# A graph layer and an expert layer on one core: norm sums moved to VectorE, rank sums added in DRAM, five chunk buffers instead of six

## The chip, the cores and the metric

The kernel runs on one core of a Trainium2 chip. The metric is device time in microseconds of that core. A core has five engines with instruction queues of their own: PE (TensorE: matmuls), DVE (VectorE), ACT (ScalarE), POOL (GpSimd) and SP (SyncE, which issues transfers here and computes nothing). An engine runs its queue in order; engines wait for one another through semaphores. DMA engines, 16 of them, move data between DRAM and the on-chip buffer (SBUF).

## The reference

`x` is 10000 x 128, `adj` is 10000 x 10000, both float32, and two layers follow each other, each added to `x`:

```
h = item_feat @ W_item.T + b_item
x = x + relu(adj @ h + layernorm(x) @ W_user.T + b_user)
z = layernorm(x)
probs = softmax(z @ gate_w + gate_b)          # 8 experts, the best two of each row count
x = x + sum over the two: prob * (gelu(z @ W1[e] + b1[e]) @ W2[e] + b2[e])
```

`adj` alone is 400 MB, and it is read once. The hidden width of an expert is 256.

## The kernel before, in words

**Blocks and chunks.** The 10000 rows of the result are cut into 20 blocks (`BLOCKS`) of 500 rows, a block's 9984 columns of `adj` into 26 chunks (`CH`) of 3 x 128. The loop variable n runs over all 520 chunks (`NCH`), c = n % 26 is the chunk in its block, and every engine's program is this one loop with small work hung into it at fixed places. A chunk is 750 KB. SP loads it into one of six buffers (`raw`, `load_raw`), which is free again when VectorE has subtracted the chunk that was in it six chunks ago (`lo_made`). ScalarE rounds it to a short format (`a_hi`, L742, three buffers), VectorE makes the rest, `a_lo = raw - a_hi` (L952, two buffers), and TensorE adds nine matmuls of 500 columns into one bank: hi x h_hi, hi x h_lo, lo x h_hi (L496, L497, L501). A short matmul for the last columns (L510) and one for the user weights (L512) end a block.

**Small work behind a block.** While block b is summed, block b-1 is finished, at places named by constants (`X1_AT` = 1, `BN2_AT` = 4, `LG_AT` = 11, ...): relu and residual (L977), turning into token order, statistics (`stats1`, `stats2`, L971 and L987), the factors of both norms (`rs`, made on Pool by `rstd`, eleven small instructions L1304 to L1320, the last but two a power of -1/2), the norms on ScalarE (L758, L787), gate logits on VectorE (L998 to L1006), the power of the softmax on Pool (L1324), the two best experts (`top`), and a slot for each row and rank (`slots`). `bn` and `rs` have one buffer.

**Scatter, fill, tiles, send.** Blocks 0 to 16 go the sparse way. Pool scatters each block's rows to expert order in DRAM (`zs`), eight indirect DMAs of 125 rows (L1346). Blocks 0 to 11 are group 0, blocks 12 to 16 group 1. When a group is scattered, VectorE writes a table of tiles, SP fills the ends of the experts' regions (`fill_end`, L379, waits for all of the group's scatters), and then 31 and 17 tiles of 512 rows (`NTG`) go through the expert's two matmul layers between the chunks. A tile's load (`load_zt`, L352) waits for the fills; its weights come by `load_w`. At a tile's end Pool sends its rows, scaled by their probability, to DRAM (`rr`, four indirect DMAs, L1355); VectorE waits with the output of tile k until the sends of tile k-2 have landed. The tiles start at `W1_AT`: the first one of group 0 at chunk 352.

**Dense steps.** Blocks 17 to 19 are run through all eight experts after the last chunk, 24 steps d with no sorting: first layer, GELU on ScalarE (L857), a scaling by the gate on VectorE (L1172), rounding (L866), rest (L1176), second layer. The GELU's output has two buffers (`dg`).

**Combine.** `out_s` holds the sparse blocks' residual, `rr` each row's two ranks. For each of the 17 sparse blocks SP loads 512 rows of `out_s` into SBUF (`comb_load`), Pool adds both ranks by accumulating DMAs (`comb_add`, L1336), and SP stores it (`comb_store`, L367). All this stands after the last chunk, beside the dense steps, and SP's `out_store` of the dense blocks (L372) stands in the same queue.

Of the kernel before, what the change touches and what calls it, by code (L numbers as in the profile page):

```python
# [23 lines left out]
RAW, HIS, LOS = 6, 3, 2  # L24
# [51 lines left out]
W_LOAD = [0, 0] + [w + (6 if o + 2 < NTG[0] else 4) for o, w in enumerate(W1_AT[:NT - 2])] + [NCH - 3, NCH - 2]  # L76
ZT_LOAD = [0, 0] + [max(W1_AT[k - 2] + 3, FILL_AT[k >= NTG[0]] + E // 2) for k in range(2, NT)]
COMB_AT = [p if p < GROUPS[1][0] else p + 3 for p in range(S)]
COMB_OUT = [6 + p if p < GROUPS[1][0] else p + 10 for p in range(S)]
# [22 lines left out]
def build(nc, adj, adj_tail, x_tok, x_t, feat_t, feat_tail, wi_t, bb, bsel_d, wu_t, gate_w, gate_b,  # L102
          w12, b12, b2, ident_d, tri_d, w8_d, base_d, dest_d, sel_d, ints_d, out_s, out_d, zs, rr):
    ctx = ExitStack()
    with ctx:
# [27 lines left out]
        bias = sb("bias", [P, 4, 3])  # L133
# [35 lines left out]
        consts = sb("consts", [P, 4, 2 * SUBS])  # L169
# [5 lines left out]
        tsl = sb("tsl", [P, 2, SUBS, E])  # L175
        idx = sb("idx", [P, 2 * SUBS], I32)
# [36 lines left out]
        bn1_made, bn2_made, rs_step, rs_made = sem("bn1_made"), sem("bn2_made"), sem("rs_step"), sem("rs_made")  # L213
        ln1_normed, ln1_turned, ln1_copied, ln2_normed = (
# [31 lines left out]
        def dg(d):  # L246
            return g[:, 0:2 * UB] if d % 2 else flat[:, 0:2 * UB]
# [47 lines left out]
        def _(sp):  # L295
# [31 lines left out]
            def load_w(o):  # L327
# [27 lines left out]

            def comb_load(p):
                if p == 0:
                    sp.wait_ge(lo_made, NCH)
                    sp.wait_ge(x1_stored, 16 * S)
                if p >= CB:  # L360
                    sp.wait_ge(comb_stored[p % CB], 16 * (p // CB))
                sp.dma_start(comb(p), out_s[p * T:(p + 1) * T, :].rearrange("(p s) d -> p (s d)", s=SUBS))\
                    .then_inc(comb_loaded[p % CB], 16)

            def comb_store(p):
                sp.wait_ge(comb_added[p % CB], 32 * (p // CB + 1))
                sp.dma_start(out_s[p * T:(p + 1) * T, :].rearrange("(p s) d -> p (s d)", s=SUBS), comb(p))\  # L367
                    .then_inc(comb_stored[p % CB], 16)
# [19 lines left out]
            for n in range(NCH):  # L388
# [57 lines left out]
            for j in range(ND + 5):  # L446
                for p in range(S):
                    if COMB_OUT[p] == j:
                        comb_store(p)
                for p in range(S):  # L450
                    if COMB_AT[p] == j:
                        comb_load(p)
# [5 lines left out]
            for i in range(CB):  # L458
                sp.wait_ge(comb_stored[i], 16 * ((S - 1 - i) // CB + 1))
# [275 lines left out]
        def _(act):  # L735
# [84 lines left out]
            def gelu(k):  # L820
# [3 lines left out]
                for h in range(2):  # L824
                    fn(g[:, h * T:(h + 1) * T], hid[h][:, :], ACT.Gelu, bias=bias[:, k % 4, h:h + 1])\  # L825
# [8 lines left out]
            def y_evac(k):  # L834
# [3 lines left out]
                fn(yt[:, :], y[0][:, :], ACT.Identity, bias=bias[:, k % 4, 2:3]).then_inc(yt_made, 1)  # L838
# [9 lines left out]
            def dense_gelu(d):  # L848
# [5 lines left out]
                if d >= 2:  # L854
                    act.wait_ge(gl_made, o - 1)
# [89 lines left out]
        def _(dve):  # L945
# [34 lines left out]
            def stats2(p):  # L980
# [7 lines left out]
                last.then_inc(bn2_made, 1)  # L988

# [231 lines left out]
            for n in range(LAST):  # L1221
# [3 lines left out]
                if b == 0:  # L1225
# [6 lines left out]
                    if c == 8:  # L1232
# [4 lines left out]
                        nc.vector.tensor_copy(base[:, :], base0[:, 0:E]).then_inc(base_set, 1)  # L1237
                    if c == 16:
# [244 lines left out]
```

## Time and profile before

| | |
|---|---|
| median of 3 runs | 1539.0 us (1538.3 to 1539.04) |
| the profiled execution | 1538.6 us, span 1536.8 us |
| PE busy, DVE busy | 1469.6 us (96%), 1248.4 us (81%) |
| ACT busy, POOL busy | 1095.3 us (71%), 885.7 us (58%) |
| moved by DMA | 498.06 MB, mean 324 GB/s |

The span runs from the first to the last instruction; what lies around it is 1.8 us. Busy time of PE is modelled at the ends of matmuls, which overlap: a matmul's row says 0.39 us while the next one starts 0.23 us after it. So idle time of TensorE is read from the distance between the starts of rows, not from its busy share.

### The profile page before, as it was taken

Reading aid. Unit: us, or ns where it says so; the run is one execution under the profiler, and the core shown is the slowest. Engines: PE = TensorE matmul, PEld = TensorE weight load, DVE = VectorE, ACT = ScalarE, POOL = GpSimd, SP = SyncE. Lnnn points to the kernel's source line nnn. Section 1 sums busy time; section 2 is a strip of 40 time slices with the busy share of each in tenths; the row PEclk is TensorE's granted clock in tenths of the full one; section 3 lists DMA queues with packets and bytes.
Section 4 is the critical chain, followed back from the end, with each engine's and each line's share of the span. In section 5 each row is a group of like instructions: output and inputs, shape, how many; then the busy total and the mean of one; then the engine's idle time right before and its main releaser. Section 6 shows DMA issues by size and latency. Waiting matters only on the chain.

```text
span 1536.8 us, 20551 instructions
## 1 busy us (share of the span) xinstructions
PE 1469.6 (96%) x6682; PEld 1172.5 (76%) x6682; DVE 1248.4 (81%) x1627; ACT 1095.3 (71%) x1162; POOL 885.7 (58%) x630
## 2 busy tenths in 40 slices
PE   8999999999999999999998798999999999999997
PEld 6777787877877877778776587888888887877664
DVE  4778788888887887888888687889898988888775
ACT  4567677677677676776774677788887878788664
POOL 0105735637557457456364148777887887587662
PEclk9999999999999999999999899999999999999999
DMA  8879999999999999999997987889898899888399
GB/s 327 303 302 348 366 360 361 377 345 344 378 347 354 364 345 364 363 344 384 338 350 262 371 315 271 332 327 337 327 335 326 327 338 331 287 274 283 110 219 229
DMA packets 141720, 498.06 MB, mean 324 GB/s; under 512 B 33024, under 2 KB 39120, under 8 KB 141614
## 3 DMA queue, kind: packets, MB, share of 16 engines
q1 hardware_dynamic: 119694, 466.12, 82.3%
q0 software_dynamic: 21920, 30.64, 7.6%
q8 instruction: 53, 0.87, 0.2%
q14 instruction: 53, 0.43, 0.1%
HBM read 460.22 MB, written 36.31 MB: 323 GB/s over the span
## 4 chain that ended last, share of the span: by engine, by line
PE 49%; DVE 15%; POOL 14%; issue 8%; ACT 7%; DMA 5%; SPq 2%; POOLq 0%; ACTq 0%; DVEq 0%
PE p_agg L501 13%; PE p_agg L496 11%; PE p_agg L497 11%; DVE s_a_lo L952 9%; ACT s_a_hi L742 4%; POOL s_rs L1316 3%; DMA s_raw<-rr 3%; POOL s_rs L1304 2%; POOL zs L1346 2%; POOL s_rs L1312 1%; POOL s_rs L1305 1%; PE p_hid L478 1%; PE p_hid L589 1%; PE p_hid L591 1%; PE p_hid L590 1%
## 5 line engine op out<-in xcount | busy, mean ns | idle before, releaser
L952 DVE TENSOR_TENSOR s_a_lo<-s_raw,s_a_hi 128x1500 fp32r<-128x1500 f32 x520 | 885.8, 1718 | 139.4 <-PE p_agg L501 84.4
L742 ACT ACTIVATE s_a_hi<-s_raw 128x1500 fp32r<-128x1500 f32 x520 | 750.1, 1454 | 207.9 <-PE p_agg L501 184.9
L496 PE MATMUL p_agg<-s_a_hi,s_h_hi 128*128 128x500 f32 x1560 | 630.6, 404 | 10.2 <-ACT s_a_hi L742 10.1
L497 PE MATMUL p_agg<-s_a_hi,s_h_lo 128*128 128x500 f32 x1560 | 611.7, 392 | 0.0
L501 PE MATMUL p_agg<-s_a_lo,s_h_hi 128*128 128x500 f32 x1560 | 449.3, 396 | 33.9 <-DVE s_a_lo L952 31.0
L1346 POOL DMA_INDIRECT zs<-s_rows,s_idx x136 | 231.9, 1705 | 306.3 <-DVE s_idx L1080 211.8
L501 PEld LDWEIGHTS p_agg<-s_a_lo,s_h_hi 128*128 128x128 f32 x1560 | 290.2, 190 | 120.2 <-DVE s_a_lo L952 63.3
L496 PEld LDWEIGHTS p_agg<-s_a_hi,s_h_hi 128*128 128x128 f32 x1560 | 297.4, 191 | 75.3 <-ACT s_a_hi L742 17.9
L497 PEld LDWEIGHTS p_agg<-s_a_hi,s_h_lo 128*128 128x128 f32 x1560 | 297.3, 191 | 57.9 <-issue 3.2
L1355 POOL DMA_INDIRECT rr<-s_ysb,s_dests x192 | 277.4, 1445 | 102.7 <-issue 53.1
L1324 POOL TENSOR_TENSOR s_gt<-s_ebase,s_gt 125x32 f32<-125x32 f32 x20 | 130.8, 6538 | 37.2 <-DVE s_gt L1006 37.1
L1304 POOL TENSOR_TENSOR s_rs<-s_bn 125x8 f32<-125x8 f32 (+1 forms) x21 | 42.2, 2010 | 113.6 <-DVE s_bn L971 104.3
L1154 DVE TENSOR_TENSOR s_gl<-s_g,s_gh 128x1024 fp32r<-128x1024 f32 x48 | 58.8, 1226 | 51.3 <-ACT s_gh L832 51.3
L825 ACT ACTIVATE s_g<-p_hid,s_bias 128x512 f32<-128x512 f32 x96 | 60.6, 684 | 48.5 <-PE p_hid L591 48.5
L832 ACT ACTIVATE s_gh<-s_g 128x1024 fp32r<-128x1024 f32 x48 | 50.9, 1060 | 9.3 <-PE p_y L607 8.1
L1316 POOL TENSOR_TENSOR s_rs<-s_rs,s_consts 125x8 f32<-125x8 f32 (+1 forms) x21 | 55.7, 2655 | 1.6
L838 ACT ACTIVATE s_yt<-p_y,s_bias 128x512 f32<-128x512 f32 x48 | 32.6, 680 | 31.4 <-PE p_y L607 31.4
L787 ACT ACTIVATE s_rows<-p_agg,s_rs 125x128 f32<-125x128 f32 x80 | 30.0, 456 | 34.1 <-POOL s_rs L1320 34.1
L1336 POOL DMA_DIRECT2D s_raw<-rr x34 | 31.0, 1134 | 32.8 <-DMA s_raw<-out_s 16.7
L746 ACT ACTIVATE s_h_hi<-p_hid 128x384 fp32r<-128x384 f32 x26 | 12.8, 491 | 41.2 <-PE p_hid L478 41.2
L589 PE MATMUL p_hid<-s_zh,s_wt 128*128 128x512 f32 (+1 forms) x102 | 41.7, 409 | 0.4 <-ACT s_g L857 0.4
L818 ACT ACTIVATE s_zh<-p_tp 128x512 fp32r<-128x512 f32 x48 | 28.2, 587 | 19.0 <-PE p_hid L591 17.2
(214 smaller groups left out, 1478.6 us busy)
## 6 DMA issues: line engine op xcount, KB each, us to landing
s_raw<-adj SPq DMA_DIRECT2D x520, 750.0 KB, 6.6
s_wraw<-w SPq DMA_DIRECT2D x56, 256.0 KB
s_zt<-zs SPq DMA_DIRECT2D x48, 264.0 KB, 3.1
s_raw<-rr POOLq DMA_DIRECT2D x34, 256.0 KB, 6.7
s_xtok<-x_tok SPq DMA_DIRECT2D x20, 256.0 KB, 5.6
s_xt<-x_t SPq DMA_DIRECT2D x20, 250.0 KB, 6.7
zs<-s_early SPq DMA_DIRECT2D x18, 264.0 KB, 5.7
out_s<-s_x1s SPq DMA_DIRECT2D x17, 256.0 KB, 6.5
```

What stands on the lines that cost most here:

```text
L496: mm(o, h_hi[:, k * D:(k + 1) * D], hi, start=(k == 0), stop=False)
L497: mm(o, h_lo[:, k * D:(k + 1) * D], hi, start=False, stop=False)
L501: last = mm(o, h_hi[:, k * D:(k + 1) * D], a_lo[:, n % LOS, j * UB:(j + 1) * UB], start=False, stop=False)
L742: fn(a_hi[:, n % HIS, :], raw[:, n % RAW, :], ACT.Copy).then_inc(hi_made, 1)
L825: fn(g[:, h * T:(h + 1) * T], hid[h][:, :], ACT.Gelu, bias=bias[:, k % 4, h:h + 1])\
L952: tt(a_lo[:, n % LOS, :], raw[:, n % RAW, :], a_hi[:, n % HIS, :].bitcast(F32), ALU.subtract)\
L1154: tt(gl[:, :], g[:, :], gh[:, :].bitcast(F32), ALU.subtract).then_inc(gl_made, 1)
L1304: tt(row[0], even, odd, ALU.add)
L1316: tt(row[1], row[5], mhalf, ALU.pow).then_inc(rs_step, 1)
L1324: gp.tensor_tensor(gt[0:TS, 2, :], ebase[0:TS, :], gt[0:TS, 1, :], ALU.pow).then_inc(ez_made, 1)
L1346: gp.indirect_dma_start(out=zs[:, :], out_offset=bass.IndirectOffsetOnAxis(ap=idx[0:TS, j:j + 1].bitcast(U32), axis=0), in_=rows[k][0:TS, ...
L1355: gp.indirect_dma_start(out=rr[:, :], out_offset=bass.IndirectOffsetOnAxis(ap=dests[:, k % XR, s:s + 1].bitcast(U32), axis=0), in_=yrows(k ...
```

## The change

Seven things are changed at once.

1. `RAW` goes from 6 to 5, and the kernel is built with 8192 instead of 4096 bytes for the descriptors that Pool writes.
2. `rstd` is split. VectorE makes the variance in six instructions (`variances`, chunk 4) and the shift in one (`shifts`, chunk 7); Pool makes only the power (`power_of_rs`).
3. The small work stands three to four chunks earlier: logits at 8 instead of 11, softmax at 12 instead of 16, slots and scatter at 17 instead of 21.
4. Fills start two chunks earlier, the first tile of group 0 five chunks earlier (347 instead of 352); the steps between tiles of group 1 are 2.41 chunks instead of 2.12. The tiles' biases have six buffers instead of four, and the loads of weights and rows stand at other chunks.
5. Scatters take 128 rows instead of 125. The three more go to spare rows of `zs`, whose numbers a new input `idx` holds.
6. The combine doesn't go through SBUF. Pool adds `rr` onto `out_s` in DRAM, two blocks of group 0 to a DMA, six DMAs for each rank, issued behind the sends of twelve tiles of group 1; group 1 follows at the end in two DMAs of five blocks.
7. The GELU's output of the dense steps has three buffers.

```diff
-RAW, HIS, LOS = 6, 3, 2
+RAW, HIS, LOS = 5, 3, 2
-X1_AT, X1T_AT, BN2_AT, BN1_AT, X1S_AT, LG_AT, LN2_AT = 1, 1, 4, 5, 4, 11, 12
-TAILHI_AT, TAILLO_AT, SOFT_AT, TOP1_AT, TOP2_AT, LN1_AT = 9, 10, 16, 17, 18, 15
-PREFIX_AT, LN1T_AT, SLOT_AT, LN1C_AT = 19, 17, 21, 20
-TABLE_AT = (21, 22, 23)
+X1_AT, X1T_AT, X1S_AT, BN1_AT, BN2_AT, FIN_AT, LG_AT, LN2_AT = 1, 1, 4, 3, 4, 7, 8, 9
+TAILHI_AT, TAILLO_AT, SOFT_AT, TOP1_AT, TOP2_AT, LN1_AT = 6, 7, 12, 13, 14, 11
+PREFIX_AT, LN1T_AT, SLOT_AT, LN1C_AT = 15, 13, 17, 16
+TABLE_AT = (17, 18, 19)
-FILL_AT = [(hi + 1) * CH + 6 for lo, hi in GROUPS]
-FIRST_W1 = [at + E // 2 + 4 for at in FILL_AT]
+FILL_AT = [(hi + 1) * CH + 4 for lo, hi in GROUPS]
+FIRST_W1 = [at + E // 2 + 1 for at in FILL_AT]
...
+            def variances(j):
+                lo, hi = SUBS if j == 0 else 0, SUBS if j == BLOCKS else 2 * SUBS
+                if j < BLOCKS:
+                    dve.wait_ge(bn1_made, j + 1)
+                if j >= 1:
+                    dve.wait_ge(bn2_made, j)
+                row = [rs[0:TS, i, lo:hi] for i in range(RS)]
+                even, odd = bn[0:TS, lo:hi, 1], bn[0:TS, lo:hi, 4]
+                tt(row[3], even, odd, ALU.subtract)
+                tt(row[4], bn[0:TS, lo:hi, 2], bn[0:TS, lo:hi, 5], ALU.add)
+                tt(row[0], even, odd, ALU.add).then_inc(rs_step, 1)
+                dve.wait_ge(rs_step, 2 * j + 1)
+                nc.vector.tensor_scalar(row[4], row[4], 1.0 / D, EPS, ALU.mult, ALU.add)
+                nc.vector.scalar_tensor_tensor(out=row[3], in0=row[3], scalar=0.25, in1=row[3],
+                                               op0=ALU.mult, op1=ALU.mult).then_inc(rs_step, 1)
+                dve.wait_ge(rs_step, 2 * j + 2)
+                tt(row[5], row[3], row[4], ALU.add).then_inc(var_made, 1)
+            def shifts(j):
...
+                dve.wait_ge(pow_made, j + 1)
...
-            def rstd(j):
...
+            def power_of_rs(j):
...
+                gp.tensor_tensor(rs[0:TS, 1, lo:hi], rs[0:TS, 5, lo:hi], mhalf[0:TS, lo:hi], ALU.pow)\
+                    .then_inc(pow_made, 1)
...
+            def add_rank(i, k):
+                blocks = GROUPS[0][1] // PAIRS
+                first, last = (i * blocks, (i + 1) * blocks) if i < PAIRS else GROUPS[1]
+                if k == 0:
+                    pool.wait_ge(rr_zeroed, 16 * 3)
+                    pool.wait_ge(x1_stored, 16 * last)
+                    for j in range(2):
+                        pool.wait_ge(sent[j], 16 * SUBS * tiles_of(j, NTG[0] if i < PAIRS else NT))
+                else:
+                    pool.wait_ge(rank0_added, 16 * (PAIRS + (i == PAIRS)))
...
+                gp.dma_start(out, new, max_dma_last_dim=8192, accum_op=ALU.add).then_inc((rank0_added, rank1_added)[k], 16)
...
             def dg(d):
-                return g[:, 0:2 * UB] if d % 2 else flat[:, 0:2 * UB]
+                return (flat[:, 0:2 * UB], g[:, 0:2 * UB], flat[:, 2 * UB:4 * UB])[d % 3]
...
-                if d >= 2:
-                    act.wait_ge(gl_made, o - 1)
+                if d >= 3:
+                    act.wait_ge(gl_made, o - 2)
...
-                            in_=rows[k][0:TS, s, :], in_offset=None).then_inc(scattered, 16)
+                            in_=rows[k][:, s, :], in_offset=None).then_inc(scattered, 16)
...
                         send(k)
-                        if k == NT - 3:
-                            rstd(BLOCKS)
+                        i = k - NTG[0] - 1
+                        if 0 <= i < 2 * PAIRS:
+                            add_rank(i % PAIRS, i // PAIRS)
+            power_of_rs(BLOCKS)
+            power(BLOCKS - 1)
+            add_rank(PAIRS, 0)
+            add_rank(PAIRS, 1)
...
-    nc = bacc.Bacc("TRN2", target_bir_lowering=False, num_devices=1, dynamic_dma_scratch_size=4096)
+    nc = bacc.Bacc("TRN2", target_bir_lowering=False, num_devices=1, dynamic_dma_scratch_size=8192)
```

## Rows read from the trace of the kernel before

**Rows 1.** Windows: us, busy (x) PE PEld DVE ACT POOL, PEclk, DMA share, GB/s

```profile
402.00:461.70 59.70, 57.55 (x261) 46.48 (x260) 50.37 (x61) 42.21 (x38) 33.88 (x21) 1.00 0.96 358
406.00:426.00 20.00, 20.00 (x97) 16.82 (x96) 17.39 (x19) 14.38 (x12) 15.89 (x13) 1.00 0.99 377
...
1433.50:1536.80 103.30, 88.98 (x346) 58.56 (x345) 68.43 (x88) 59.33 (x87) 51.02 (x56) 0.97 0.83 199
840.00:864.00 24.00, 14.89 (x48) 10.30 (x46) 8.72 (x6) 6.64 (x6) 4.55 (x11) 0.86 0.97 342
```

**Rows 2.** Waits: engine and line, releaser: us in total, times, longest us

```profile
POOL zs L1346 <- issue: 94.2, 121, 6.5
POOL rr L1355 <- issue: 53.1, 174, 0.6
...
DVE s_gt L998 <- POOL s_rs L1320: 26.3, 12, 2.2
ACT s_a_hi L742 <- DMA s_raw<-adj: 22.1, 8, 8.7
```

**Rows 3.** Timeline: start us, duration us, engine, line; the ends of two blocks

```profile
401.40 0.39 PE L510 MATMUL p_agg<-s_tail_parts,s_h_tail 96*128 96x500 f32 x1
...
461.53 0.39 PE L510 MATMUL p_agg<-s_tail_parts,s_h_tail 96*128 96x500 f32 x1
```

**Rows 4.** Timeline of TensorE's last third of chunks, and of the logits between

```profile
425.49 0.84 PE L501 MATMUL p_agg<-s_a_lo,s_h_hi 128*128 128x500 f32 x3
427.53 0.84 PE L501 MATMUL p_agg<-s_a_lo,s_h_hi 128*128 128x500 f32 x3
...
428.79 0.19 DVE L998 TENSOR_TENSOR s_gt<-p_small,s_rs 125x32 f32<-125x32 f32 x1 [2.20 <-POOL s_rs L1320]
...
436.19 0.83 PE L501 MATMUL p_agg<-s_a_lo,s_h_hi 128*128 128x500 f32 x3
```

**Rows 5.** Timeline of SP's queue and of Pool around the first fills

```profile
820.61 5.99 SPq L299 DMA_DIRECT2D s_raw<-adj  x4
...
823.99 3.32 POOL L1346 DMA_INDIRECT zs<-s_rows,s_idx  x1 [5.71 <-issue]
...
838.73 1.49 SPq L379 DMA_DIRECT2D zs<-s_early  x2
...
850.04 0.48 SPq L299 DMA_DIRECT2D s_raw<-adj  x1
...
858.05 9.20 SPq L299 DMA_DIRECT2D s_raw<-adj  x7
```

**Rows 6.** Timeline of VectorE in block 14

```profile
927.93 0.69 DVE L1161 TENSOR_TENSOR s_ysb<-p_y,s_probs 128x512 f32<-128x512 f32 x1 [5.80 <-DMA rr<-s_ysb,s_dests]
```

**Rows 7.** Timeline of ScalarE, two dense steps

```profile
1506.53 1.25 ACT L857 ACTIVATE s_g<-p_hid,s_dbias 128x500 f32<-128x500 f32 x2 [1.50 <-DVE s_h_hi L1176]
...
1510.21 1.24 ACT L857 ACTIVATE s_raw<-p_hid,s_dbias 128x500 f32<-128x500 f32 x2 [1.50 <-DVE s_h_hi L1176]
```

**Rows 8.** Timeline of the end

```profile
1527.91 0.68 DVE L1181 TENSOR_TENSOR s_xt<-p_y,s_xt 128x500 f32<-128x500 f32 x1 [1.88 <-PE p_y L664]
...
1533.97 0.43 SPq L372 DMA_DIRECT2D out_d<-s_xt  x1
```

**Rows 9.** Page: groups (busy us, mean ns, idle), DMA issues (KB, us to landing)

```profile
L952 DVE TENSOR_TENSOR s_a_lo<-s_raw,s_a_hi 128x1500 fp32r<-128x1500 f32 x520 | 885.8, 1718 | 139.4 <-PE p_agg L501 84.4
L742 ACT ACTIVATE s_a_hi<-s_raw 128x1500 fp32r<-128x1500 f32 x520 | 750.1, 1454 | 207.9 <-PE p_agg L501 184.9
...
L1346 POOL DMA_INDIRECT zs<-s_rows,s_idx x136 | 231.9, 1705 | 306.3 <-DVE s_idx L1080 211.8
...
L1355 POOL DMA_INDIRECT rr<-s_ysb,s_dests x192 | 277.4, 1445 | 102.7 <-issue 53.1
...
s_raw<-adj SPq DMA_DIRECT2D x520, 750.0 KB, 6.6
...
s_raw<-rr POOLq DMA_DIRECT2D x34, 256.0 KB, 6.7
```

More of the change, by code:

```diff
@@ L75 @@
 SPLIT_AT = [w - (1 if o < NT else 2) for o, w in enumerate(W1_AT)]
[L76 to L79, printed above, removed]
+W_LOAD = [0, 0] + [w + 5 for w in W1_AT[:NT - 2]] + [NCH - 3, NCH - 2]
+ZT_LOAD = [0, 0] + [max(W1_AT[k - 2] + 5, FILL_AT[k >= NTG[0]] + E // 2) for k in range(2, NT)]
 LAST = NCH + ND + 5
@@ L445, in _ @@
             load_w(NT + 3)
[L446 to L452, printed above, removed]
+            for j in range(ND + 4):
                 if j + 4 < E:
@@ L457, in _ @@
             sp.wait_ge(stored, 16 * (BLOCKS - S))
-            for i in range(CB):
-                sp.wait_ge(comb_stored[i], 16 * ((S - 1 - i) // CB + 1))
+            sp.wait_ge(rank0_added, 16 * (PAIRS + 1))
+            sp.wait_ge(rank1_added, 16 * (PAIRS + 1))
         @block.tensor
@@ L1243, in _ @@
                             .then_inc(b2_split, 1)
+                if n < NCH and c == BN1_AT + (4 if b == 0 else 0):
+                    stats1(b)
                 if b >= 1 and n < NCH:
@@ L1246, in _ @@
                 if n < NCH:
-                    if c == BN1_AT + (4 if b == 0 else 0):
-                        stats1(b)
+                    if c == BN2_AT + (3 if b == 0 else 0):
+                        variances(b)
+                    if c == FIN_AT + (3 if b == 0 else 0):
+                        shifts(b)
                     if c == TAILLO_AT:
@@ L1270, in _ @@
                     stats2(BLOCKS - 1)
+                    variances(BLOCKS)
+                if d == 4:
+                    shifts(BLOCKS)
                 if d == 3:
@@ L1324, in power @@
                 gp.tensor_tensor(gt[0:TS, 2, :], ebase[0:TS, :], gt[0:TS, 1, :], ALU.pow).then_inc(ez_made, 1)
[L1326 to L1327 removed]
+            def add_rank(i, k):
+                blocks = GROUPS[0][1] // PAIRS
+                first, last = (i * blocks, (i + 1) * blocks) if i < PAIRS else GROUPS[1]
+                if k == 0:
                     pool.wait_ge(rr_zeroed, 16 * 3)
[L1329 to L1337 removed]
+                    pool.wait_ge(x1_stored, 16 * last)
[3 more added lines that the diff above has]
+                    pool.wait_ge(rank0_added, 16 * (PAIRS + (i == PAIRS)))
+                rows_of = slice(first * T, last * T), slice(k * RANK + first * T, k * RANK + last * T)
+                out, new = (t[rows, :].rearrange("(p s) d -> p (s d)", p=P) for t, rows in zip((out_s, rr), rows_of))
+                gp.dma_start(out, new, max_dma_last_dim=8192, accum_op=ALU.add).then_inc((rank0_added, rank1_added)[k], 16)
             def scatter(p):
@@ L1360, in _ @@
             gp.memset(ones[:, :], 1.0).then_inc(sets, 1)
-            for i, value in enumerate((1.0 / D, 0.25, EPS, -0.5)):
-                gp.memset(consts[:, i, :], value)
+            gp.memset(mhalf[:, :], -0.5)
             gp.memset(ebase[:, :], 2.718281828459045).then_inc(sets, 1)
@@ L1394, in _ @@
                         send(k)
-                        if k == NT - 3:
-                            rstd(BLOCKS)
-            for first, last in ((0, GROUPS[1][0]), (GROUPS[1][0], S)):
-                for p in range(first, last + 2):
-                    if p < last:
-                        comb_add(p, 0)
-                    if p - 2 >= first:
-                        comb_add(p - 2, 1)
-                    if p == 4:
-                        power(BLOCKS - 1)
+                        i = k - NTG[0] - 1
[5 more added lines that the diff above has]
+            add_rank(PAIRS, 1)
 def kernel(**inputs):
```

111 lines of the change are left out of this document (39 added, 72 removed).

## The prediction

> **What bounds the kernel now.** I read the table of stages first. In one block of the first stretch TensorE is busy 57.6 of 59.7 us while the DMA engines are busy 0.96 of the time and move 358 GB/s [rows 1]: two resources stand side by side, so the next view has to say which one waits. The list of waits answers: ScalarE waited for an adjacency load only 8 times, 22.1 us in all [rows 2]. So TensorE sets the pace and the loads keep up, though not by much. Then the boundaries: the tail matmul of a block stands at 401.40 and the next at 461.53, so a block takes 60.13 us [rows 3]. Undisturbed, one chunk takes 2.04 us (425.49 to 427.53); 26 are 53.0 us, the other 7.1 us are transposes, gate, prefix, block end and stalls. One stall is plain in the timeline: from 427.53 to 436.19 three chunks take 8.66 us instead of 6.12, so 2.5 us are lost, and it starts where VectorE stands 2.20 us for Pool's last rs instruction (L998 behind L1320) [rows 4]. That wait occurred 12 times, 26.3 us [rows 2]: nearly every block of the first stretch has it.
>
> Blocks 13 to 19 carry the expert tiles as well. There I looked for single large stalls. The queue of the raw loads stands still twice in block 13: from 826.60 until the first fill at 838.73 (12.1 us, it waits for the last scatter of group 0), and from 850.52 to 858.05 (fills not landed) [rows 5]. In 840 to 864 TensorE is busy 14.9 of 24 us, at a granted clock of 0.86 (part of it at 1.2 instead of 2.4 GHz) [rows 1]. One more is in block 14: VectorE 5.80 us for a send that stands behind a scatter on Pool [rows 6].
>
> At the end 24 dense steps run at 3.68 us each (1506.53 to 1510.21), each opening with ScalarE waiting 1.50 us for VectorE's L1176 [rows 7]; the last out_d store leaves at 1533.97 although its data was ready at 1528.59 [rows 8], since SP first waits for the combine's stores.
>
> **The change, part by part.** All sums are against the profiled execution, 1538.6 us (span 1536.8); the median of the runs is 1539.0, so 0.4 more.
>
> *rs on VectorE, Pool keeps only the power.* Pool loses ten instructions per block and keeps one. VectorE gains seven of the size of L998, 0.19 us [rows 4]: 1.3 us per block. The power is due at chunk 4 and read at chunk 7, six us later; logits at chunk 8 read a value VectorE itself wrote. So the 2.5 us stall should go: 12 blocks x 2.5 = 30 us. What comes late next: VectorE's cushion is small, since a subtraction takes 1.72 us [rows 9] of a chunk's 2.04 [rows 4], leaving 0.32 us. At chunk 4 the second statistics and the six variance instructions stand together, at chunk 8 four logits instructions; I charge 0.6 us per block for it (half of the 1.3 us), 7 us. The added wait is shifts' for Pool's power; behind it queue the subtractions, then TensorE. It costs nothing while Pool is free for 6 us; where Pool is amid sends it may cost the old 2.2 us.
>
> *Five raw buffers.* A buffer's round is 6.6 us from issue to landing [rows 9], 1.45 us rounding (L742), 1.72 us subtraction, and some 0.6 us between them (estimated): 10.4 us. Six buffers allow 1.73 us per chunk, five 2.08, and the block would need 57.6 / 26 = 2.22 on average. So five suffice on average and fail where landing is slow (scatters under way). I take 0.3 us per block, 4 us in the first stretch. Bounds: 0, and 12 us (1 us per block).
> A rule of the Trainium skill speaks against any gain here: its page DMA: Bandwidth & Descriptors (section Bandwidth) puts the HBM-side limit of a core at about 358 GB/s, which is exactly what the whole block moves. By that rule the blocks could not shorten. The row of 406 to 426 holds 377 GB/s over 20 us [rows 1], so I go by the row, and keep the case as a rival.
> First stretch: 30 - 7 - 4 = 19 us saved; bounds 0 to 30.
>
> *Scatters and their order.* Scatters start four chunks earlier, fills two chunks earlier, and with five buffers SP arrives at them one chunk later: three chunks gained, 6.1 us. Scatters of 125 rows stall once in a set, here 5.71 us of issue gap [rows 5]; over the kernel their gaps sum to 94.2 us in 121 while 174 gaps of the 128-row sends sum to 53.1 with none over 0.6 [rows 2]. Full 128 rows and the larger descriptor space should take that away: 5.4 us more. Then 0.26 us on each of eight (the two L rows' means, 1.71 and 1.45 [rows 9]): 2.1. Together 13.6 us against a wait of 12.1: the first standstill goes. The second stays (a zt load behind unlanded fills), and five buffers cover one chunk less of it. I take 8 us saved in block 13; bounds 2 (the gaps stay) and 12.
>
> *Blocks 14 to 19.* The first send now stands ahead of the scatter on Pool, not behind it: the 5.80 us wait goes, less what TensorE had covered, 4 us. Pool has ten instructions per block less and no wait at VectorE. More bias buffers, later w and zt loads hold SP less; but five buffers reach less far when SP waits. I take 2 us for all of that, so 6; bounds -6 (1 us per block lost to the fifth buffer) and 12.
>
> *Adding the ranks in DRAM.* 12 of the 14 DMAs run during the tiles of group 1, where the DMA engines have room: the last stretch moves 199 GB/s on average [rows 1], and SP loses 34 issues. Price: Pool's issue, some 1.1 us each, behind a send. What no row shows is the accumulate of DRAM into DRAM. Nearest is s_raw<-rr, 256 KB in 6.7 us [rows 9]. The last two move 1.25 MB each, one after the other: at the rate of 377 GB/s 3.5 us, at five times 6.7 us 33.5. I take 12 us each, nearer to the low end since these descriptors go out together. They start after the softmax power of the last block, whose logits stand at dense step 6: about 7 steps of 3.6 us and 7 us for the power (estimated), so 32 us after the last chunk. The dense steps last until 24 x 3.25 + 6 = 84, the stores until 87: even 24 us are hidden. At 33.5 each the adds end at 99, 12 us after everything else.
>
> *Three dense buffers.* GELU of step d now waits for the subtraction of d-2, not d-1, so the ring of 3.68 us opens. Next is TensorE: 12 matmuls at 0.227 us (2.04 / 9) are 2.72, the broadcast and its restart about 0.45: 3.2 us. I take 3.25: 23 x 0.43 = 10 us; bounds 3 and 12.
>
> *The end.* SP no longer stands at the combine's stores: the out_d store leaves 5.4 us earlier (1533.97 to 1528.59). I take 5; bounds 3 and 5.4.
>
> Nothing: the idx copy (once), mhalf, the loads' extra tensor; they are single instructions of under 1 us in block 0, where TensorE waits for features.
>
> Sum: 19 + 8 + 6 + 0 + 10 + 5 = 48 us; 1538.6 - 48 = 1490.6, by the median 1491.
>
> **Rivals.**
> *A. The loads bind in the first stretch.* A block's bytes take 0.96 x 60.13 = 57.7 us of DMA time as they run now, and a shallower queue keeps the engines less busy; then freed TensorE time turns into waits of ScalarE for s_raw. For it: 0.96 and 358 GB/s. Against: 377 GB/s over 20 us and 22.1 us of such waits in all. Price: the 19 us, so 1510.
> *B. The DRAM adds end last.* Pool and DMA tail of two serial 1.25 MB adds. For it: the present combine chain is DMA latency, 6.7 us per 256 KB. Against: fewer, larger DMAs and 50 us of cover. Price 12 us: 1503.
> *C. The fifth buffer costs more than all gains: slower.* Place: ScalarE's wait for s_raw<-adj, in all 520 chunks. The round over five buffers is (landing + 3.8) / 5. Without this charge the other gains are 52 us and a chunk of the first stretch takes 2.24 us (2.31 less 23 / 312). They are eaten when its 312 chunks lose 0.17 us each, at 2.41 us per chunk, so from a mean landing of 8.2 us on, against 6.6 now. At 8.4 us the loss is 62 us and the time 1549. For it: landing rises when scatters and other loads queue, and SP waits in order. Against: with fewer loads in flight each lands sooner.
> *D. The stall merely moves.* VectorE's seven instructions and the closer order of its small work cost as much as Pool's wait did; the standstills of block 13 stay: 1538.6 - 6 - 10 - 5 = 1518.
>
> **How the numbers follow.** Forecast 0.60 (1491, its own range 1472 to 1505), A 0.18, B 0.06, C 0.06, D 0.10. Low end: all upper bounds are 30 + 12 + 12 + 12 + 5.4, about 1467. High end: D's 1518 with a little, 1521. Anything within 0.2% (3 us) of the time before counts as no change; only the space between D and C gives that, 0.02. Faster 0.93, slower 0.05.
>
> **What would show it.** Right: no wait of VectorE for Pool at the logits; blocks 1 to 12 near 58.5 us with over 365 GB/s; ScalarE's waits for s_raw<-adj grown, but under 60 us; no issue gaps of 5 us among the scatters; the fill right after its raw load in block 13; dense steps of 3.2 to 3.3 us; out_d stored within 1 us of its data. Wrong: blocks of 60 us with the engines at 0.98 (A); rank adds as the end of the chain (B); waits for s_raw<-adj over 70 us (C); TensorE waiting for L952's successor at chunks 4, 8 and 13 (D).

## The result and the profile after

The changed kernel takes 1515.4 us (median of 4 runs, 1513.5 to 1519.5) against 1538.65 us of the kernel before on the same chip: ratio 0.9856, 95% interval 0.9831 to 0.9880. It is faster by 23 us. The forecast was 48 us (1491, its own range 1472 to 1505; the wide range 1467 to 1521 holds the time).

To see where the rest went I cut every profiled execution at the tail matmuls that end blocks 0, 12 and 19. The times of these rows give four stretches, which are used from here on (us):

| kernel | block 0 | blocks 1-12 | blocks 13-19 | after the last chunk | span |
|---|---|---|---|---|---|
| before | 100.5 | 725.4 | 607.5 | 103.5 | 1536.8 |
| changed | 97.1 | 705.0 | 621.0 | 91.7 | 1514.8 |
| difference | -3.4 | -20.4 | +13.5 | -11.8 | -22.0 |
| forecast | 0 | -19 | -14 | -15 | -48 |

Blocks 1 to 12 and the last stretch do about what was forecast. Blocks 13 to 19, the tile stretch, were to give 14 us and cost 13.5. That is the whole miss. The 3.4 us in block 0 hardly come from the change: one more trace of the kernel before with nothing changed in this block (dense3 below) has 97.3 there.

**Blocks 1 to 12.** Windows of the changed kernel: an undisturbed block, one that waited for loads, and the last stretch (columns as in rows 1).

```profile
449.70:507.60 57.90, 57.47 (x264) 46.70 (x262) 51.46 (x68) 42.14 (x39) 24.42 (x10) 1.00 0.97 371
565.70:625.50 59.80, 58.72 (x263) 46.37 (x262) 51.67 (x69) 42.68 (x38) 25.01 (x10) 1.00 0.97 362
1423.11:1514.80 91.69, 85.65 (x347) 60.05 (x345) 68.86 (x95) 59.27 (x87) 18.21 (x13) 0.99 0.24 56
```

A block takes 57.9 us where nothing is late, against 60.13 before [rows 3], and moves 371 GB/s; five of the twelve take 57.9 to 58.0, the others 58.7 to 59.8. The prediction quoted a page of the Trainium skill, DMA: Bandwidth & Descriptors (section Bandwidth), which puts a core's HBM-side limit at about 358 GB/s. By it these blocks could not have become shorter; the trace does not agree, whole blocks run at 371 here. The prediction left out a condition of that same section: it gives about 358 GB/s as what each core gets with both cores of a pair streaming, and more for a core that streams alone. This program runs on one core; what the other core of its pair did, no run here shows. So the figure, as quoted, was no bound on this kernel.

The waits of the changed kernel (engine and line, releaser: us in total, times, longest):

```profile
ACT s_a_hi L717 <- DMA s_raw<-adj: 97.9, 120, 5.0
...
POOL zs L1342 <- issue: 52.3, 124, 14.7
...
PEld p_tp L555 <- DMA s_zt<-zs: 18.3, 7, 5.1
...
PE p_tp L555 <- DMA s_zt<-zs: 14.2, 6, 4.6
```

VectorE's wait for Pool at the logits [rows 2] is gone. ScalarE now waits 120 times for a chunk, 97.9 us, where it waited 8 times and 22.1 us [rows 2]. Pool's longest wait by "issue" before a scatter, 14.7 us, is no gap between two scatters: it stands ahead of block 8's set, where the other sets of blocks 1 to 12 wait 12.7 to 14.6 us for VectorE's slots. And TensorE waits for the load of a tile's rows (L555 is the turning of a tile), a wait that the list of before does not have at all.

**Blocks 13 to 19.** The deltas of the single blocks are +2.9, -6.8, -0.6, +0.9, +1.0, +14.6 and +1.6 us. Block 14, whose 5.80 us wait of VectorE [rows 6] is gone, gains more than forecast. Block 18, in which group 1's tiles start, loses 14.6 us. Its two ends in the timeline of TensorE, 103.57 us apart (89.0 before), and the first tile's turn of each group:

```profile
829.07 1.11 PE L555 MATMUL p_tp<-s_ident,s_zt 128*128 128x128 f32 x4 [4.57 <-DMA s_zt<-zs]
...
1212.63 0.39 PE L485 MATMUL p_agg<-s_tail_parts,s_h_tail 96*128 96x500 f32 x1
...
1240.38 0.95 PE L555 MATMUL p_tp<-s_ident,s_zt 128*128 128x128 f32 x4 [4.08 <-DMA s_zt<-zs]
...
1316.20 0.39 PE L485 MATMUL p_agg<-s_tail_parts,s_h_tail 96*128 96x500 f32 x1
```

These deltas also hold work that moved, for the first tiles start five chunks earlier. Windows of blocks 13, 18 and 19, first of the kernel before, then of the changed one (columns as in rows 1):

```profile
825.87:909.84 83.97, 72.91 (x316) 57.52 (x315) 58.87 (x82) 54.38 (x58) 26.45 (x22) 0.94 0.84 310
1238.99:1328.00 89.01, 87.58 (x421) 71.51 (x419) 76.61 (x113) 70.86 (x86) 62.02 (x45) 1.00 0.93 326
1328.00:1433.32 105.32, 102.99 (x503) 82.74 (x502) 88.47 (x127) 84.46 (x108) 80.76 (x63) 1.00 0.76 255
```

```profile
802.10:889.01 86.91, 77.17 (x342) 61.95 (x341) 65.39 (x96) 60.52 (x66) 29.90 (x19) 0.94 0.91 327
1212.63:1316.20 103.57, 93.10 (x430) 75.03 (x429) 78.86 (x119) 72.45 (x89) 59.50 (x41) 0.97 0.90 306
1316.20:1423.11 106.91, 98.39 (x472) 78.08 (x471) 84.02 (x126) 78.02 (x99) 77.42 (x56) 1.00 0.90 283
```

Block 13 has 26 matmuls more, and the part of it in which TensorE isn't busy is 9.7 us where it was 11.1. Block 19 has 31 fewer and is longer all the same: TensorE isn't busy for 8.5 us where it was 2.3. In block 18 it is 10.5 us for 1.4. Over blocks 13 to 19 together the number of matmuls is the same (2780 and 2781), so the stretch can be compared as a whole, its single blocks only with these counts.

Pool and SP around the first fills, the counterpart of rows 5:

```profile
782.71 1.10 POOL L1342 DMA_INDIRECT zs<-s_rows,s_idx  x1 [13.12 <-DVE s_idx L1085]
...
789.81 5.36 POOL L1342 DMA_INDIRECT zs<-s_rows,s_idx  x1 [0.30 <-issue]
...
792.89 7.98 SPq L293 DMA_DIRECT2D s_raw<-adj  x5
807.23 1.50 SPq L359 DMA_DIRECT2D zs<-s_early  x2
...
817.73 0.47 SPq L293 DMA_DIRECT2D s_raw<-adj  x1
...
824.54 1.44 SPq L346 DMA_DIRECT2D s_zt<-zs  x2
826.02 1.69 SPq L293 DMA_DIRECT2D s_raw<-adj  x2
```

SP still stands at the first fill, from 800.87 to 807.23 (6.4 us instead of 12.1 [rows 5]), and no raw load leaves between 818.2 and 826.02. The gaps of 5.7 us between scatters are gone, but one scatter itself now takes 5.36 us, and from the first scatter to the first fill it is 24.5 us (24.4 before: its first scatter stands at 814.36, the fill at 838.73). Issuing the set takes 18.6 us instead of 21.2, but the fill follows the end of the last issue by 5.9 us instead of 3.2. The tile's rows are asked for at 824.5 and wanted at 824.5: TensorE stands until 829.07.

**The end.** Two dense steps on ScalarE and the last rows of VectorE and SP:

```profile
1498.15 1.25 ACT L832 ACTIVATE s_raw<-p_hid,s_dbias 128x500 f32<-128x500 f32 x2 [1.14 <-PE p_hid L566]
...
1501.52 1.25 ACT L832 ACTIVATE s_g<-p_hid,s_dbias 128x500 f32<-128x500 f32 x2 [1.20 <-PE p_hid L566]
...
1504.85 1.25 ACT L832 ACTIVATE s_raw<-p_hid,s_dbias 128x500 f32<-128x500 f32 x2 [1.15 <-PE p_hid L566]
...
1511.53 0.68 DVE L1186 TENSOR_TENSOR s_xt<-p_y,s_xt 128x500 f32<-128x500 f32 x1 [1.89 <-PE p_y L639]
...
1512.23 0.33 SPq L352 DMA_DIRECT2D out_d<-s_xt  x1
```

Most steps take 3.33 to 3.37 us, some 3.6 to 3.8 (3.68 before [rows 7]), and their release is TensorE. The last store leaves as soon as its data is there. The two large additions in DRAM on Pool's timeline:

```profile
1456.62 1.00 POOL L1333 DMA_DIRECT2D out_s<-rr  x1
1466.13 0.86 POOL L1333 DMA_DIRECT2D out_s<-rr  x1 [8.51 <-DMA out_s<-rr]
```

The first 1.25 MB are added in 9.5 us. The second addition is issued 49 us ahead of the end, and from 1480 on the DMA engines are idle for 10 us: both are hidden.

### The profile page after: what moved, and what is told of

Read it like the earlier page. It is cut to its first block, busy times and chain, and to the rows that moved or that the text cites. A ratio compares the mean times of both kernels' runs of the same rounds, so it can differ in the third digit from the quotient of the medians.

```text
span 1514.8 us, 20455 instructions
## 1 busy us (share of the span) xinstructions
PE 1460.2 (96%) x6682; PEld 1166.5 (77%) x6682; DVE 1263.8 (83%) x1775; ACT 1095.4 (72%) x1162; POOL 709.0 (47%) x397
## 4 chain that ended last, share of the span: by engine, by line
PE 64%; DVE 13%; issue 7%; DMA 6%; ACT 5%; SPq 3%; POOL 2%; DVEq 0%; ACTq 0%; POOLq 0%
PE p_agg L476 16%; PE p_agg L471 15%; PE p_agg L472 14%; DVE s_a_lo L927 9%; ACT s_a_hi L717 3%; DMA s_raw<-adj 2%; POOL zs L1342 2%; PE p_hid L564 2%; PE p_hid L566 2%; PE p_hid L565 2%; DMA s_zt<-zs 2%; ACT s_xtok L733 1%; PE p_hid L453 1%; PE p_agg L487 1%; PE p_tp L555 1%
## 5 line engine op out<-in xcount | busy, mean ns | idle before, releaser
L476 PE MATMUL p_agg<-s_a_lo,s_h_hi 128*128 128x500 f32 x1560 | 448.1, 395 | 16.2 <-DVE s_a_lo L927 11.8
L476 PEld LDWEIGHTS p_agg<-s_a_lo,s_h_hi 128*128 128x128 f32 x1560 | 286.9, 189 | 104.8 <-DVE s_a_lo L927 49.0
L1351 POOL DMA_INDIRECT rr<-s_ysb,s_dests x192 | 270.7, 1410 | 176.4 <-DVE s_ysb L1166 124.0
L1342 POOL DMA_INDIRECT zs<-s_rows,s_idx x136 | 236.3, 1738 | 203.8 <-DVE s_idx L1085 151.5
L1313 POOL TENSOR_TENSOR s_rs<-s_rs,s_mhalf 125x8 f32<-125x8 f32 (+1 forms) x21 | 55.4, 2637 | 240.3 <-DVE s_rs L982 240.2
L807 ACT ACTIVATE s_gh<-s_g 128x1024 fp32r<-128x1024 f32 x48 | 51.0, 1062 | 18.8 <-PE p_y L582 14.7
L555 PE MATMUL p_tp<-s_ident,s_zt 128*128 128x128 f32 x192 | 30.1, 280 | 18.8 <-DMA s_zt<-zs 14.2
L555 PEld LDWEIGHTS p_tp<-s_ident,s_zt 128*128 128x128 f32 x192 | 22.9, 143 | 25.0 <-DMA s_zt<-zs 18.3
L566 PE MATMUL p_hid<-s_zl,s_wt 128*128 128x512 f32 (+1 forms) x102 | 40.4, 396 | 0.0
L1144 DVE TENSOR_TENSOR s_zl<-p_tp,s_zh 128x512 fp32r<-128x512 f32 x48 | 32.8, 684 | 9.0 <-ACT s_zh L793 8.8
```

Source lines behind the costliest of these rows:

```text
L476: last = mm(o, h_hi[:, k * D:(k + 1) * D], a_lo[:, n % LOS, j * UB:(j + 1) * UB], start=False, stop=False)
L555: last = nc.tensor.transpose(tp[:, s * P:(s + 1) * P], zt[:, k % 2, s, 0:D], ident[:, :])
L566: last = mm(hid[h][:, 0:n], w_hi, lo, start=False, stop=True)
L1342: gp.indirect_dma_start(out=zs[:, :], out_offset=bass.IndirectOffsetOnAxis(ap=idx[:, j:j + 1].bitcast(U32), axis=0), in_=rows[k][:, s, :], ...
L1351: gp.indirect_dma_start(out=rr[:, :], out_offset=bass.IndirectOffsetOnAxis(ap=dests[:, k % XR, s:s + 1].bitcast(U32), axis=0), in_=yrows(k ...
```

## The experiments

Each kernel was timed beside the kernel before on the same chip, whose medians were 1538.4, 1535.2 and 1535.4 us in three sets of kernels. So kernels of different sets are compared by their ratio to it.

**First question: the places of the tile loads.** SP's program leads TensorE by as many chunks as there are chunk buffers. `ZT_LOAD` went from +3 to +5 behind a tile two earlier, while that lead fell from six to five: a load inside a group is issued three chunks later than before. A group's first tiles are loaded at a place of their own, `FILL_AT` + 4, which the +2 does not move; but the first tile now stands 5 chunks behind the fill's place, not 8, so with the lost buffer its load has four chunks less.

*zt3: the changed kernel with the loads back at +3.*

```diff
-ZT_LOAD = ... max(W1_AT[k - 2] + 5, ...)
+ZT_LOAD = ... max(W1_AT[k - 2] + 3, ...)
```

> Only the place of the tile loads changes: ZT_LOAD is W1_AT[k-2] + 3 again, as before the change, instead of + 5. Theory T (the tile loads come too late: in the changed kernel TensorE waits at L555 for s_zt in blocks 13, 18 and 19, some 21 us of idle time): in group 1 the load then leads its use by four chunks instead of two, the waits of tiles 32 to 47 go, the two first ones of a group (4.6 and 4.1 us) stay: 10 to 13 us faster than the changed kernel, about 1503. Theory B (the fifth raw buffer is what costs, and the tile waits only show it): no gain, 1512 to 1518.

Measured: 1511.3 us, ratio 0.9825 (0.9789 to 0.9860). Blocks 13 to 19 take 615.9 us. That is a third of the gain that theory T expected, and the time alone lies nearer to theory B. The waits decide: the small ones at L555 go and two, 6.0 and 5.3 us, remain, the groups' first tiles:

```profile
PE p_tp L555 <- DMA s_zt<-zs: 11.3, 2, 6.0
```

*first4: the changed kernel with the first tile three chunks later.*

```diff
-FIRST_W1 = [at + E // 2 + 1 for at in FILL_AT]
+FIRST_W1 = [at + E // 2 + 4 for at in FILL_AT]
```

> Only the first tile of each group moves back: FIRST_W1 is 4 chunks behind the fills again instead of 1, so tiles start at chunk 350 and 480. Theory T: the waits of 4.6 and 4.1 us of each group's first tile go, the later ones of group 1 stay or grow a little, since the tiles stand 2.24 instead of 2.41 chunks apart: 6 to 10 us faster than the changed kernel, about 1507. Theory B: no gain.

Measured: 1520.7 us, ratio 0.9887 (0.9862 to 0.9912): a miss. Blocks 13 to 19 take 622.4 us. The first tiles no longer wait, but with a later start and the same end group 1's tiles follow every 2.24 chunks, not every 2.41, and the load at +5 has that much less lead: 11.6 us of idle time at L555 turned up, 3.8 in block 18 and 7.7 in block 19.

*both: the two together.*

> The two edits together (tile loads at + 3, first tile 4 chunks behind the fills). Theory T: nearly all of the 21 us of TensorE's idle time at L555 goes, 16 to 21 us faster than the changed kernel, 1494 to 1499. Theory B: within 3 us of the changed kernel's 1515.

Measured: 1500.2 us, ratio 0.9743 (0.9718 to 0.9768), 15 us under the changed kernel and 1 us above the expected range; blocks 13 to 19 take 606.3 us and L555 waits for no load. Block 18 gives back 12.6 us of its 14.6 and block 19 4.3; block 13, with 14 matmuls fewer in it, only 0.9. Each half alone gives 4 us, which the intervals do not separate from nothing, or nothing, for the other half's wait takes its place.

**Second question: the fifth buffer and the descriptor space.**

*raw6: the changed kernel with six chunk buffers and 4 KB for Pool's descriptors.*

```diff
-RAW, HIS, LOS = 5, 3, 2
+RAW, HIS, LOS = 6, 3, 2
-    nc = ...(..., dynamic_dma_scratch_size=8192)
+    nc = ...(..., dynamic_dma_scratch_size=4096)
```

> The changed kernel with six raw buffers, and 4096 bytes of descriptors to make room. Theory B: 20 us or more faster, 1495 or less, ScalarE's waits for s_raw<-adj back from 98 to about 22 us, and the tile stretch (blocks 13 to 19) 15 us or more shorter. Theory T: blocks 1 to 12 gain about 0.6 us each (7 us), the tile loads lead by one chunk more and TensorE's 21 us at L555 shrink by a third to a half: 1500 to 1504.

Measured: 1503.6 us, ratio 0.9770 (0.9745 to 0.9795). 8.5 us come in blocks 1 to 12 (696.5), 5.1 in the tiles. Its list of waits:

```profile
ACT s_a_hi L717 <- DMA s_raw<-adj: 16.4, 10, 5.1
```

*scratch4: the changed kernel, five buffers, 4 KB.*

> The changed kernel with 4096 instead of 8192 bytes for Pool's descriptors. If the larger space took away the scatters' issue gaps (as the prediction had it): gaps of 5 us come back, blocks 13 and 18 longer by 3 to 6 us, 1519 to 1525. If it does nothing (the 128-row scatters took the gaps away, or nothing that TensorE waits for hangs on them): within 3 us of the changed kernel's 1515.

Measured: 1518.6 us, ratio 0.9881 (0.9842 to 0.9920), which overlaps the changed kernel's; the stretches are 704.8, 622.2 and 91.8. The larger space gives nothing that can be measured in the time. In the trace it does something: two gaps inside a set are back.

```profile
326.86 2.27 POOL L1342 DMA_INDIRECT zs<-s_rows,s_idx  x1 [5.89 <-issue]
```

```profile
738.92 1.95 POOL L1342 DMA_INDIRECT zs<-s_rows,s_idx  x1 [6.31 <-issue]
```

So of the 17 sets of a run ten have a gap of over 5 us with 125 rows and 4 KB (before, rs_alone), two with 128 rows and 4 KB (scratch4, raw6, places), none with 128 rows and 8 KB. The two fall in blocks 4 and 11, where nothing that TensorE needs waits for them. 125 rows with 8 KB was not run.

**Third question: which parts carry the gain.**

*rs_alone: the kernel before, with variances and shifts on VectorE right behind its own statistics (chunks 5 and 8).*

```diff
                     if c == BN1_AT + (4 if b == 0 else 0):
                         stats1(b)
+                        variances(b)
+                    if c == BN1_AT + 3 + (4 if b == 0 else 0):
+                        shifts(b)
```

> The kernel before with one part of the change: VectorE makes the variances (behind its statistics at chunk 5) and the shift (chunk 8), Pool only the power. Six buffers and all other places as before. Theory R (the prediction's: the stall at chunk 12 is Pool's eleven instructions): VectorE's wait at L998 goes, the 12 blocks of the first stretch lose 2 to 2.5 us each, 20 to 30 us faster than the kernel before. Rival D (the seven instructions cost VectorE as much): under 6 us.

Measured: 1503.4 us, ratio 0.9794 (0.9768 to 0.9820). This one part gives 32 us, more than the whole change. Blocks 1 to 12 take 692.7 us, and VectorE's wait for Pool at the logits is gone from the list. One of them in the windows:

```profile
443.47:501.03 57.56, 57.23 (x262) 46.97 (x261) 51.23 (x68) 42.45 (x38) 25.36 (x11) 1.00 1.00 375
```

*dense3: the kernel before with three buffers for the GELU's output.*

```diff
-                return g[:, 0:2 * UB] if d % 2 else flat[:, 0:2 * UB]
+                return (flat[:, 0:2 * UB], g[:, 0:2 * UB], ...)[d % 3]
-                if d >= 2:
-                    act.wait_ge(gl_made, o - 1)
+                if d >= 3:
+                    act.wait_ge(gl_made, o - 2)
```

> The kernel before with a third buffer for the GELU's output of the dense steps, nothing else. Theory E (two chains end together, the combine's transfers hide what the steps gain): steps fall from 3.68 to about 3.3 us, but the last out_d store still leaves behind the combine's stores, 0 to 3 us faster than before. Rival (the steps alone set the end): 8 us faster.

Measured: 1537.5 us, ratio 1.0012 (1.0001 to 1.0024): no gain, though the steps fall to some 3.3 us. The combine sets the end there: the last rows are ready at 1524.61, and their store waits in SP's queue until 1532.35.

```profile
1523.93 0.68 DVE L1181 TENSOR_TENSOR s_xt<-p_y,s_xt 128x500 f32<-128x500 f32 x1 [1.87 <-PE p_y L664]
...
1532.35 0.43 SPq L372 DMA_DIRECT2D out_d<-s_xt  x1
```

*dense2: the changed kernel with two such buffers.*

> The changed kernel with two activation buffers instead of three in the dense stretch; all else as changed. Theory E (the dense steps took 3.33 us instead of 3.68 us only when both the third buffer is there and Pool's additions no longer share the stretch): the steps go back to 3.6 to 3.7 us, 24 of them, so the time is 6 to 9 us above the changed kernel's, 1522 to 1525 us. Rival F (the gain came from Pool's 34 additions leaving alone; the third buffer alone did nothing in the old kernel): the steps stay at 3.3 to 3.4 us and the time stays at 1513 to 1519 us.

Measured: 1524.0 us, ratio 0.9916 (0.9895 to 0.9937), 0.6% or 9 us above the changed kernel. The last stretch takes 98.7 us instead of 91.7, and the steps are those of before, with the same releaser:

```profile
1508.50 1.25 ACT L832 ACTIVATE s_g<-p_hid,s_dbias 128x500 f32<-128x500 f32 x2 [1.51 <-DVE s_h_hi L1181]
...
1512.18 1.25 ACT L832 ACTIVATE s_raw<-p_hid,s_dbias 128x500 f32<-128x500 f32 x2 [1.51 <-DVE s_h_hi L1181]
```

So the third buffer is worth 7 to 9 us, but only once the combine has left the end.

**Fourth question: a kernel that keeps the parts and drops the loss.**

*best: both and raw6 together.*

> The changed kernel with tile loads at + 3, the first tile 4 chunks behind the fills, six raw buffers and 4096 bytes of descriptors: the two gains measured singly (15 us for the places, 12 us for the buffer, 5 of these in the tile stretch and partly the same). Theory T and B both hold and add up where they don't overlap: 1488 to 1493, blocks 13 to 19 together near 602 us, blocks 1 to 12 near 697. If they are one effect: 1497 to 1501.

Measured: 1495.3 us, ratio 0.9735 (0.9712 to 0.9758), 2 us above the expected range. Blocks 1 to 12 take 696.7 us, 4 us more than with rs_alone, though ScalarE hardly waits for loads there any more. Blocks 13 to 19 take 608.4 us, where 602 was expected and both had 606.3: beside the mended places the sixth buffer gives nothing in the tile stretch.

*late: best with the fill at place 7 instead of 4.*

```diff
-FILL_AT = [(hi + 1) * CH + 4 for lo, hi in GROUPS]
+FILL_AT = [(hi + 1) * CH + 7 for lo, hi in GROUPS]
```

> The changed kernel with six chunk buffers and 4 KB for Pool's descriptors, zt loads at +3, the first tile 8 places behind the fill, and now the fill at place 7 instead of 4. Theory L (from the start of the last scatter set before a fill to the fill it is 24.4 us whatever the order; SP stands 6 us at the fill because its place comes too early): SP stands under 1 us at the first fill, block 13 takes 80 to 82 us instead of 84.6, and the time is 3 to 6 us under that of the same kernel with the fill at place 4 (1495 us): 1489 to 1492. Rival M (what is late there is only moved: the tiles start 3 chunks later and their steps are shorter, which costs as much in blocks 14 to 19): 1494 to 1499.

Measured: 1496.1 us, ratio 0.9735 (0.9715 to 0.9755), the same time as best. SP's row of raw loads now reaches almost to the fill, and it stands 2.3 us:

```profile
782.90 13.34 SPq L293 DMA_DIRECT2D s_raw<-adj  x8
798.54 1.84 SPq L359 DMA_DIRECT2D zs<-s_early  x2
```

Block 13 takes 74.2 us instead of 83.4 (12 matmuls fewer stand in it), and the whole tile stretch 597.3 instead of 608.4. But the last stretch takes 104.1 instead of 91.9, so nothing is left. Theory L named the mechanism and missed the time, M the reverse: the loss is not in blocks 14 to 19, it is behind the last chunk (below).

*places: every part of the change but five buffers and 8 KB, with all places as before the change.*

```diff
-X1_AT, X1T_AT, X1S_AT, BN1_AT, BN2_AT, FIN_AT, LG_AT, LN2_AT = 1, 1, 4, 3, 4, 7, 8, 9
+X1_AT, X1T_AT, BN2_AT, BN1_AT, FIN_AT, X1S_AT, LG_AT, LN2_AT = 1, 1, 4, 5, 8, 4, 11, 12
...                    # SOFT_AT 16, SLOT_AT 21, FILL_AT +6, FIRST_W1 +4, W_LOAD +6/+4, ZT_LOAD +3, RAW 6
```

> Norm sums and shifts on VectorE, rank sums by additions in DRAM, three activation buffers, six biases, scatters of 128 rows; but six chunk buffers, 4 KB for Pool's descriptors, and every place (small work, fill, first tile, w and zt loads) as before the change. Theory T (the new places and the fifth buffer's loss are all that took the gain away): the first stretch as with the norm sums alone on VectorE (692 us in blocks 1 to 12), tiles 609, tail 91 to 94 instead of 101: 1491 to 1496 us. Rival D (the additions in DRAM cost the tile stretch something that the new places had hidden): tiles 613 or more, 1498 to 1503 us.

Measured: 1489.5 us (1486.7 to 1491.6), ratio 0.9695 (0.9676 to 0.9713). It beats both kernels: 3.1% under the kernel before. Stretches 692.7, 598.6 and 99.1. The time is 1.5 us under theory T's range, but not as T had it: the tile stretch is 10 us shorter than expected and the last stretch 5 us or more longer. Rival D is refuted.

*places5: the same with five chunk buffers.*

> The same as the run with all old places, with five chunk buffers instead of six. Theory T: blocks 1 to 12 lose what six buffers won on the changed kernel (8 us there), the tile stretch little, since the zt loads are back at +3: 1500 to 1506 us, that is 7 to 12 us above the run with six. Rival G (the old, later places of the small work made five buffers enough; the raw waits come from the new places): within 3 us of the run with six.

Measured: 1501.5 us, ratio 0.9786 (0.9766 to 0.9806). Stretches 703.0, 599.4 and 99.0. The waits of the two, places first:

```profile
ACT s_a_hi L717 <- DMA s_raw<-adj: 17.7, 7, 6.3
```

```profile
ACT s_a_hi L717 <- DMA s_raw<-adj: 120.8, 140, 6.8
```

One buffer is 12 us, 10.3 of them in blocks 1 to 12 and 0.8 in the tiles. And since places5 differs from the changed kernel in places and descriptor space alone, and scratch4 shows no effect of the space on this stretch (622.2), the new places are what costs 621.0 - 599.4 = 21.6 us of the tile stretch.

The stretches of all runs beside the first table (us):

| kernel | 1-12 | 13-19 | last | ratio |
|---|---|---|---|---|
| zt3 | 703.7 | 615.9 | 94.6 | 0.9825 |
| first4 | 703.1 | 622.4 | 91.9 | 0.9887 |
| both | 706.0 | 606.3 | 91.7 | 0.9743 |
| raw6 | 696.5 | 615.9 | 91.7 | 0.9770 |
| scratch4 | 704.8 | 622.2 | 91.8 | 0.9881 |
| rs_alone | 692.7 | 609.5 | 101.3 | 0.9794 |
| dense3 | 724.6 | 608.2 | 105.4 | 1.0012 |
| dense2 | 705.3 | 622.7 | 98.7 | 0.9916 |
| best | 696.7 | 608.4 | 91.9 | 0.9735 |
| late | 696.8 | 597.3 | 104.1 | 0.9735 |
| places | 692.7 | 598.6 | 99.1 | 0.9695 |
| places5 | 703.0 | 599.4 | 99.0 | 0.9786 |

## Why the prediction was wrong, step by step

**rs on VectorE, 30 less 7: right, a little low.** With nothing else changed it gives 32.7 us in blocks 1 to 12 (rs_alone), so Pool's late factor was indeed the stall, and VectorE has room for seven small instructions a block. The charge of 7 us belongs to the closer places alone, and is 4 us there (696.7 of best against 692.7).

**The fifth buffer, 4 us: the mechanism was right, the size was off.** It costs 8.5 us in blocks 1 to 12 at the new places (705.0 against raw6's 696.5) and 10.3 at the old ones, inside the bound of 12. The text set 2.08 us per chunk allowed against 2.22 needed on the average of a block. But its own row has 2.04 us for an undisturbed chunk, which is shorter than the 2.08 us, so by the text's own numbers the loads had to fall behind in an undisturbed run of chunks; and landing times are no average either. The sum of the stretch came out right (19 against 20.4) because this error and the one above cancel.

**Block 13, "I take 8 us saved in block 13": wrong, it lost 2.9.** The three chunks of order were gained (SP stands 6.4 us instead of 12.1). The 5.4 us of issue gaps were not: the gap went, but one scatter stretched to 5.36 us, and the set needs as long as before until the fill. Of the time won at the fill 4.57 us were given back at the first tile's turn. And the text did not count that a tile that starts five chunks earlier brings 26 matmuls into this block, 4.3 us of busy TensorE. Less this work the block saved 1.3 us, not 8.

**Blocks 14 to 19, "More bias buffers, later w and zt loads hold SP less ... I take 2 us for all of that": this is the step that failed.** I put a later load down as relief for SP and never asked when the tile needs it. Places and buffers are counted in the same unit: a load is issued (place - buffers) chunks after the start, so inside a group +2 in the place and -1 in the buffers are three chunks, 6 us and more. A group's first tile lost four: three because it is used that much sooner behind the fill, one by the buffer. Before, its rows were asked for 12.1 and 11.2 us ahead of their turn (856.57 to 868.65 in the first group, 1265.62 to 1276.81 in the second); in the changed kernel it is 4.5 and 2.8 us, all of it spent waiting. In place of the 6 us forecast as a gain blocks 14 to 19 lost 10.6. zt3, first4 and both show that the loads' place and the first tile's place must be mended together; both gets 14.7 us back in the tile stretch, and all places together 21.6. What of these 21.6 the small work's places and the weight loads have is not separated. The other half of the step held in size: block 14 gained 6.8 us for the 4 forecast. Its reason, the first send ahead of the scatter, is not what it takes: places has the scatter first again, and block 14 takes the same 80.7 us with no such wait. Its set is issued in 12.5 us where the kernel before took 20.5 with a gap of 5.69 us in it. rs_alone, with 125 rows and a gap of 5.88 us in that set, still has the wait (5.6 us) and 86.3 us.

**DRAM additions, nothing: right.** Landing took 9.5 us for the 12 assumed. **Dense steps, 10, and the end, 5: nearly right,** 11.8 us for both; the step is mostly 3.33 us where I took 3.25. The two terms do not stand alone, though: without the combine's move the third buffer gives nothing (dense3), and with it 7.0 of the 11.8 (dense2).

**Rivals.** A (loads bind) shows in the waits but not in the time, B did not happen, C had the right place and a fifth of its price (12 us of 62). D's "the standstills of block 13 stay" came true in part, but not its stall at VectorE. None of the rivals had the wait for s_zt; that D's number, 1518, lies nearest is an accident.

**Still open.** In places, places5 and late the second dense step starts late: ScalarE stands although TensorE's matmuls for it ended at 1394.8, and the profile names no engine that it waited for. In places:

```profile
1391.20 1.25 ACT L832 ACTIVATE s_raw<-p_hid,s_dbias 128x500 f32<-128x500 f32 x2 [1.22 <-PE p_hid L566]
...
1398.97 1.25 ACT L832 ACTIVATE s_g<-p_hid,s_dbias 128x500 f32<-128x500 f32 x2 [6.01 <-remote]
```

In late it is 11.0 us and in places5 8.1. The late step is followed by a lower clock; the windows of the last stretch of places and of late:

```profile
1388.57:1487.60 99.03, 90.87 (x347) 63.71 (x345) 68.95 (x95) 59.38 (x87) 17.90 (x14) 0.93 0.23 55
```

```profile
1391.30:1495.40 104.10, 90.99 (x347) 63.84 (x345) 68.94 (x95) 59.33 (x87) 18.81 (x15) 0.90 0.22 52
```

The granted clock is 0.93 and 0.90 where the changed kernel has 0.99, and the stretch is 7 and 12 us longer than there. The wait and the lower clock come together in these runs, and in places, the fastest kernel, too: some of its 99.1 us could still be had. Pool has eight more sends to issue at this point, but so it has in the changed kernel and in best, which do not stand there: the sends alone don't explain it, and it was not tested further. Also open: which of the wider scatters, the additions in DRAM and the six bias buffers gives places its 10.9 us in blocks 13 to 19 over rs_alone. 5.6 of them are in block 14, where the trace points at the scatters (above); 4.4 are in block 13. And of the 27.5 us between the forecast and the result of this stretch the runs place 14.7 at the tile loads and the first tile; the rest is only known to lie in block 13 and in the other places.

## What to carry to other kernels

Where an issuing queue runs ahead of the compute by its number of buffers, every place in it is relative to that number. Taking a buffer away moves all its other loads later by one step; work out for each load, and first for the first one of a phase, how long before its use it is issued. Moving work also moves what a block's time contains: compare stretches with the same work in them. A part that pays alone (32 us here) can hide that its companions lose: undo them one at a time, and in pairs, because two waits in one chain hide each other.

## What was not expected of the hardware

- A core moved 371 to 375 GB/s over whole blocks of 58 us, at a DMA share of 0.97 to 1.00.
- Scatters of 125 rows have an issue gap of over 5 us in ten of 17 sets, scatters of 128 rows in two (4 KB of descriptor space) or none (8 KB). A set of block 2 takes 21.2 us with the gap and 16.6 without. But in the set before the first fill one scatter takes 5.36 us, and the fill can go no earlier.
- An accumulating transfer from DRAM to DRAM handles 1.25 MB in 9.5 us, while 256 KB into SBUF took 6.7 [rows 9].
